# Expert part of a gated attention and mixture-of-experts kernel: eight row buffers, four bias buffers, transposes two tiles ahead

## The reference, cut to what matters

```
x = x + tanh(g_xattn) * gated_bidirectional_attention(layernorm(x), ctx)     # x: 8 x 512 x 512, float32
xt = layernorm(x).reshape(4096, 512)
probs = softmax(xt @ router_w + router_b)          # 8 experts
gate, idx = max(probs), argmax(probs)              # one expert for each token
y = gate * (xt @ expert_w[idx] + expert_b[idx])
out = x + tanh(g_ffn) * y
```

## Time and profile before

| | us |
|---|---|
| median of 3 runs | 1170.18 (1168.96 to 1170.37) |
| the profiled execution | 1162.84 |
| its span, first to last instruction | 1161.1 |
| PE busy | 1144.8 (99%) |
| DVE busy | 709.3 (61%) |
| ACT busy | 459.3 (40%) |
| POOL busy | 212.4 (18%) |

### The profile page before, as it was taken

The page is one execution under the profiler, slowest core; times in us unless marked ns, Lnnn a source line. Parts: engine busy times, 40 slices in busy tenths (PEclk is TensorE's granted clock), DMA queues, the critical chain, the costliest instruction groups (busy, mean ns, idle before and its releaser), DMA issues.

```text
span 1161.1 us, 18112 instructions
## 1 busy us (share of the span) xinstructions
PE 1144.8 (99%) x5933; PEld 942.6 (81%) x5933; DVE 709.3 (61%) x1494; ACT 459.3 (40%) x815; POOL 212.4 (18%) x339
## 2 busy tenths in 40 slices
PE   8999999999999999999999999999999999999988
PEld 6888888888888888888888888888888888877876
DVE  6666646564656555754576356546565658689655
ACT  5634413442344224432443134423342355554432
POOL 2400101020101100110011011101020101257754
PEclk9999999999999999999999999999999999999999
DMA  7141102010201020111101110103010312677783
GB/s 255 42 162 44 37 28 100 11 39 28 99 9 49 27 99 9 41 35 63 45 21 36 63 64 21 37 27 99 9 40 0 137 47 77 201 259 209 203 242 108
DMA packets 59444, 90.64 MB, mean 78 GB/s; under 512 B 20522, under 2 KB 21062, under 8 KB 59400
## 3 DMA queue, kind: packets, MB, share of 16 engines
q1 hardware_dynamic: 49232, 64.25, 18.2%
q0 software_dynamic: 7264, 19.20, 5.1%
q10 hardware_dynamic: 2904, 6.63, 1.6%
HBM read 62.77 MB, written 29.12 MB: 79 GB/s over the span
## 4 chain that ended last, share of the span: by engine, by line
PE 90%; issue 2%; SPq 2%; DMA 2%; DVE 2%; POOL 2%; ACT 1%; POOLq 0%; ACTq 0%; DVEq 0%
PE mm L160 59%; PE u L1049 15%; PE tr L1001 8%; PE u L160 5%; PE tr L160 1%; SPq L1579 1%; PE tr L1103 1%; DMA in_tile<-x_rows,u_row 1%; PE mm L1830 1%; SPq L1580 1%; POOL out L1659 1%; DMA probs<-in_L_ffn_expert_b 0%; DMA slot_as_f<-in_L_xattn_Wk_s 0%; DVE arena L1273 0%; DVE slot_as_f L1806 0%
## 5 line engine op out<-in xcount | busy, mean ns | idle before, releaser
L160 PE MATMUL mm<-arena 128*128 128x512 f32 x1536 | 374.1, 395 | 1.5 <-DVE arena L1273 1.4
L160 PEld LDWEIGHTS mm<-arena 128*128 128x128 f32 x1536 | 282.8, 188 | 58.5 <-DVE arena L1273 1.6
L1049 PE MATMUL u<-arena 128*128 128x512 f32 x768 | 189.8, 397 | 0.0
L160 PE MATMUL mm<-arena,q_pair 128*128 128x512 f32 x768 | 183.8, 394 | 0.0
L160 PEld LDWEIGHTS mm<-arena,q_pair 128*128 128x128 f32 x768 | 141.7, 188 | 28.7
L1049 PEld LDWEIGHTS u<-arena 128*128 128x128 f32 x768 | 140.0, 188 | 27.4
L1273 DVE TENSOR_TENSOR arena<-tr,arena 128x512 fp32r<-128x512 f32 x144 | 96.6, 685 | 36.9 <-ACT arena L1164 16.5
L1273 DVE TENSOR_TENSOR arena<-mm,arena 128x512 fp32r<-128x512 f32 x64 | 44.2, 691 | 91.4 <-ACT arena L1155 90.1
L1151 ACT ACTIVATE q_pair<-mm,c_col 128x512 fp32r<-128x512 f32 x64 | 44.1, 689 | 125.8 <-PE mm L160 122.6
L1274 DVE SCALAR_TENSOR_TENSOR q_pair<-mm,c_col,q_pair 128x512 fp32r<-128x512 f32 x64 | 48.1, 751 | 70.7 <-ACT q_pair L1151 69.0
L1155 ACT ACTIVATE arena<-mm 128x512 fp32r<-128x512 f32 x64 | 38.3, 599 | 128.8 <-PE mm L160 128.8
(11 more groups left out here) (220 smaller groups left out, 1555.8 us busy)
## 6 DMA issues: line engine op xcount, KB each, us to landing
in_tile<-in_ctx SPq DMA_DIRECT2D x31, 256.0 KB, 2.7
x_tile<-in_x SPq DMA_DIRECT2D x29, 256.0 KB, 2.6
x_rows<-x_tile SPq DMA_DIRECT2D x29, 256.0 KB, 2.1
in_tile<-in_x SPq DMA_DIRECT2D x28, 256.0 KB, 2.7
x_rows_early<-x_tile SPq DMA_DIRECT2D x28, 256.0 KB, 2.3
probs<-in_L_ffn_expert_b SPq DMA_DIRECT2D x21, 256.0 KB, 4.9
slot_as_f<-in_L_ffn_expert_w SPq DMA_DIRECT2D x4, 1024.0 KB, 5.5
slot_as_f<-in_L_ffn_expert_w ACTq DMA_DIRECT2D x3, 1024.0 KB, 7.5
```

Source lines behind the costliest of these rows:

```text
L160: last = pe.matmul(bank, lhsT(a, c), rhs(b, c), start=start and n == 0, stop=stop and n == C * len(PASSES) - 1)
L1049: last = pe.matmul(u_bank[m][:], v_pair[:, i % 2, a, tile(m)], pt_pair[:, i % 2, p], start=i == 0 and n == 0, stop=i == T - 1 and n == 2)
```

## The change

It does the following:

- Eight row buffers instead of six; the two new ones lie in `probs`, which the last batch frees with its M transposes. Four bias buffers instead of seven.
- PE transposes two tiles ahead: T(i) is transposes of i+2, then product i. In T0, T18 and T19 the transposes stand behind the product. Tile 1 is transposed in TP, ahead of the last gate product. ACT does high(i+2) and normalise(i+3), DVE low(i+2), add_bias(i), finish(i).
- POOL's gathers get an order of their own (`gathers_in_turn`): gather 6 behind scatter 1; in T2 and T3 two gathers each, in front of the scatter; then gather(i+7) up to T12; none in T13 to T15; one each in T16 and T17 (tiles 20, 21), two each in T18 to T20 (22 to 27), then again gather(i+7).
- The four list scatters of the last batch are issued in one go in RK0 (before: one there, three in steps of their own behind T10, T11 and T12). TB3 stands before T10, TB4 and TB5 before T11, TB6 and LI0 before T12.
- The late indices: four tiles in LI0, and then two tiles a step from T13, behind the step's bias (before: four a step from T15, ahead of it).
- ACT's wait for the last gate product moves from normalise(2) to the head of T0, ahead of high(1).

```
-ROWS, NORMED, PAIR, BIAS, BANK, OUT = 6, 3, 3, 7, 4, 4
+ROWS, NORMED, PAIR, BIAS, BANK, OUT = 8, 3, 3, 4, 4, 4
...
-               T6 LG1 LR1 NT2 NM3 NR2 T7 LG2 LR2 NT3 NR3 T8 LG3 LR3 RT0 IW0 T9 RK0 T10 TB3 RS1
-               T11 TB4 RS2 T12 TB5 RS3 TB6 LI0"""
+               T6 LG1 LR1 NT2 NM3 NR2 T7 LG2 LR2 NT3 NR3 T8 LG3 LR3 RT0 IW0 T9 RK0 TB3 T10 TB4 TB5
+               T11 TB6 LI0 T12"""
...
-                    for t in range(1 if after else T):
+                    for t in range(T):
                         scatter_list(t)
-                elif kind == "RS":
-                    scatter_list(i)
...
                 if i == 1:
-                    for n in range(3, BIAS):
-                        load_bias(n)
-                if FIRST_LATE < i:
-                    load_late_idx(i - FIRST_LATE)
+                    load_bias(3)
                 if i + BIAS - 1 == EARLY:
                     sp.wait_ge(experts_ready, 2)
                 if 0 < i <= TILES - BIAS:
                     load_bias(i + BIAS - 1)
+                if i >= FIRST_LATE:
+                    for n in range(2):
+                        if EARLY + LOADS + 2 * (i - FIRST_LATE) + n < TILES:
+                            load_idx(EARLY + LOADS + 2 * (i - FIRST_LATE) + n)
...
+            elif n == 6:
+                pool.wait_ge(attention.m_tr, 4 * B)
...
+        def gathers_in_turn(i):
+            if i < 2:
+                return ()
+            if i < 4:
+                return (2 * i + 3, 2 * i + 4)
+            if i < EARLY - ROWS + 1:
+                return (i + ROWS - 1,)
+            if i < EARLY - 4:
+                return ()
+            if i < EARLY - 2:
+                return (i + 4,)
+            if i < EARLY + 1:
+                return (2 * i - 14, 2 * i - 13)
+            return (i + ROWS - 1,) if i + ROWS - 1 < TILES else ()
...
-                if ROWS <= i + ROWS - 1 < TILES and i > 0:
-                    gather(i + ROWS - 1)
+                for n in gathers_in_turn(i):
+                    gather(n)
                 scatter(i)
+                if i == 1:
+                    gather(6)
...
             elif kind == "T":
-                if i + 1 < TILES:
-                    high(i + 1)
+                if i == 0:
+                    act.wait_ge(attention.g_mm, 4 * B)
+                    high(1)
+                    normalise(2)
                 if i + 2 < TILES:
-                    normalise(i + 2)
+                    high(i + 2)
+                if i + 3 < TILES:
+                    normalise(i + 3)
...
+                behind = i == 0 or EARLY <= i + 2 < EARLY + 2
...
-                if i + 1 < TILES:
-                    transpose_rows(i + 1)
+                if not behind and i + 2 < TILES:
+                    transpose_rows(i + 2)
...
+                if behind:
+                    transpose_rows(i + 2)
```

More of the change, by code:

```diff
@@ L46 @@
 EARLY = 20
-ROWS, NORMED, PAIR, BIAS, BANK, OUT = 6, 3, 3, 7, 4, 4
+ROWS, NORMED, PAIR, BIAS, BANK, OUT = 8, 3, 3, 4, 4, 4
 LOADS = 4
 SP_LOADS = 4
-FIRST_LATE = 14
+FIRST_LATE = 13
 FILLS = 5
@@ L1464, in scatter_list, with run @@
                 in_=token_ids[:, t:t + LINE], in_offset=None).then_inc(listed, 16)
-        def run(b, steps, after=False):
+        def run(b, steps):
             for kind, rel, d, i in steps:
@@ L1507, in gpsimd @@
             else:
-                run(B - 1, [step], after=True)
+                run(B - 1, [step])
     part = Part(sync, scalar, vector, gpsimd, tensor)
@@ L1555, in experts_part @@
     q, c2s, slot = k.pairs_as_f32[:, 0], k.pairs_as_f32[:, 1], attention.slot_of_gs
+    mix = attention.probs[:].rearrange("p t l -> p (t l)")
     def pair_in(whole, n):
@@ L1562, in experts_part @@
     row = [k.in_tile[:, 0], k.in_tile[:, 1], k.in_tile[:, 2], c2s[:, 4 * H:4 * H + ROWX],
-           c2s[:, 4 * H + ROWX:4 * H + 2 * ROWX], q[:, 5 * H:5 * H + ROWX]]
+           c2s[:, 4 * H + ROWX:4 * H + 2 * ROWX], q[:, 5 * H:5 * H + ROWX], mix[:, 0:ROWX], mix[:, ROWX:2 * ROWX]]
     y = [slot[:, n * H:(n + 1) * H] for n in range(OUT)]
-    bias = [c2s[:, 7 * H:8 * H], q[:, 7 * H:8 * H], slot[:, 7 * H:8 * H]] + [attention.probs[:, t] for t in range(T)]
+    bias = [c2s[:, 7 * H:8 * H], q[:, 7 * H:8 * H], slot[:, 7 * H:8 * H], mix[:, 2 * ROWX:2 * ROWX + H]]
     tr_bank, y_bank = attention.mm_bank, attention.u_bank
@@ L1581, in load_idx @@
                          ).then_inc(idx_loaded[n // LOADS], 16)
[L1583 to L1586, removed]
         def load_bias(n):
@@ L1628, in run @@
                 sp.wait_ge(attention.listed, 16 * T * B)
-                load_late_idx(0)
+                for n in range(EARLY, EARLY + LOADS):
+                    load_idx(n)
         return run
@@ L1683, in normalise @@
                 act.wait_ge(attention.gc_mm, 1)
-            elif n == 2:
-                act.wait_ge(attention.g_mm, 4 * B)
             elif n >= NORMED:
@@ L1700, in run @@
                 normalise(0)
+                normalise(1)
             elif kind == "TP":
                 high(0)
-                normalise(1)
             elif kind == "T":
-                if i + 1 < TILES:
-                    high(i + 1)
+                if i == 0:
+                    act.wait_ge(attention.g_mm, 4 * B)
+                    high(1)
+                    normalise(2)
                 if i + 2 < TILES:
-                    normalise(i + 2)
+                    high(i + 2)
+                if i + 3 < TILES:
+                    normalise(i + 3)
         return run
@@ L1814, in run @@
             elif kind == "T":
-                if i + 1 < TILES:
-                    low(i + 1)
+                if i == 0:
+                    low(1)
+                elif i + 2 < TILES:
+                    low(i + 2)
                 add_bias(i)
                 finish(i)
+                if i == 0:
+                    low(2)
         return run
@@ L1836, in run @@
                 transpose_rows(0)
+                transpose_rows(1)
             elif kind == "T":
+                behind = i == 0 or EARLY <= i + 2 < EARLY + 2
                 if i == 0:
```

## The result

The change makes the kernel slower. Beside each other on one chip, before took 1170.37 us (median of 5 runs, 1168.96 to 1171.34) and after 1175.77 us (5 runs, 1173.96 to 1178.26): a ratio of 1.0054, 95% interval 1.0039 to 1.0069. I had forecast 1169.0 us with a range of 1164.5 to 1172.6. The profiled execution of after took 1173.96 us, with a span of 1172.2.

What follows compares the result with a forecast made beforehand. PE was taken to bound the kernel, so only its gaps could be won. The terms -0.4 + 2.65 - 1.7 + 2.8 - 6.1 + 1.6 = -1.15 took 1170.18 to 1169.0 us, range 1164.5 to 1172.6.

Steps and rivals of the forecast that it cites:

- second half: From product 21 on: gathers asked for eight tiles ahead and evenly spaced biases remove the 6.1 us lost there, -6.1.
- T20: Ahead of tile 22's transposes: row 22 lands at 1093.05, PE waits 2.8 us, +2.8; row 20 comes just in time.
- Start and T1 to T5: Tile 1 transposed earlier, -0.4; early gathers on POOL delay BS1, NM1 and T5's transposes, +2.65.
- Table stretch: Low part made a tile earlier on DVE, so PE's 0.3 and 1.15 us gaps go: -1.7.
- Clock: Two new PE gaps over 2 us, near 1036 to 1039 and at 1091; one drop of the granted clock taken, +1.6.
- Rival 4: At T20 gathers 22 and 23 land late, PE waits 6.2 us, both new gaps lower the clock: 1174.0, chance 0.15.
- I take the difference over unchanged: The runs' median lies 7.3 us above the profiled execution; this was assumed the same after: 1170.18 - 1.15 = 1169.0.

Runs made afterwards that it cites:

- b_again: The kernel before, unchanged, run and profiled again: 1159.95 us, 0.9995 of before, span 1158.4.
- a_again: The kernel after, unchanged, run again beside the kernel before: 1.0036 of before, span 1163.3.
- b_third: The kernel before, unchanged, profiled a third time, in a session where it runs near 1170 us: 1.0005 of before, span 1168.5.
- a_fourth: The kernel after, unchanged, a fourth time, in a session with before near 1170 us: 1.0065 of before, span 1173.3.
- a_one_ahead: The kernel after with transposes, high and low parts one tile in advance as before, all the rest of the change kept: 1.0006 of before.
- a_back_to_one: The kernel after, but nothing transposed at T16 and one tile in advance again from T17 on: 1.0071 of before.
- b_lists_once: The kernel before with late indices two a step behind the bias, list scatters in one go and the table's parts one step earlier: 0.9983 of before.

## Why the prediction was wrong

When PE starts the transposes ahead of a product, in two pairs of profiles (b_again and a_again are from two sessions with before near 1160, b_third and a_fourth from one near 1170):

```
ahead of product       3       5      12      13      17      22      36     span
b_again            1029.9  1037.3  1063.9  1067.1  1081.4  1097.4  1144.9  1158.4
a_again            1030.4  1041.8  1067.8  1071.0  1083.8  1105.4  1150.3  1163.3
after - before        0.5     4.5     3.9     3.9     2.4     8.0     5.4     4.9
b_third            1031.0  1038.4  1067.2  1072.6  1089.2  1106.3  1155.0  1168.5
a_fourth           1031.4  1043.2  1071.2  1079.7  1094.4  1115.3  1160.3  1173.3
after - before        0.4     4.8     4.0     7.1     5.2     9.0     5.3     4.8
```

From product 3 on, after has one more tile's transposes behind it than before; the differences hold some 0.5 us for that, which the last column gives back. The difference of the spans is the same in both, 4.8 to 4.9. Two steps of the prediction failed: the size of the second half (-6.1, read from one execution), and T20, where row 20 was said to be just in time and the transposes behind the product were taken as free. Term by term, with the first pair and clock drops (1.6 each) taken out:

- **Start and T1 to T5**: forecast -0.4 + 2.65 = +2.25, measured 4.5 - 1.6 = +2.9. BS1's end was right to 0.1 us, and a_one_ahead shows that chain alone holding PE for 2.23 us. But in after it is not what PE waited for. Row 6 took 6.7 us (6.6 in a_again), above the 6 up to which I had said it hides; PE stood for it, and product 4 then covered NM1's delay. That the wait for row 6 came out as long as the one forecast for tile 7 is luck. The 0.52 us ahead of tile 3 were not in the sum.
- **Table stretch**: forecast -1.7, measured 2.4 - 4.5 = -2.1. Right in these sessions. In the pair of 1170 it was +0.4, eaten by the late answer behind the four list scatters.
- **T20**: forecast +2.8, measured 8.0 - 2.4 - 1.6 = +4.0. The step that failed here is "row 20 comes at 1086 to 1087.5 and just in time". The starts were written at 1072.8 instead of 1070.0, SP's first late index left at 1073.8 instead of 1070.7, bias 15 stood behind four of them and held DVE 2.48 us, so scatter 15 went at 1084.8 and gather 20 behind it at 1086.1 instead of 1082.65. Its row came at 1090.8. That is a chain that I had written down, with each link some 3 us too early. Of the +4.0, 1.8 are the wait for row 20 and 1.4 the change of order ahead of tile 22, which the sum had at nothing; the 2.8 forecast for row 22's landing did not come, the row was in time.
- **Clock**: one drop forecast, two here (three in the first profile): +1.6 more.
- **Second half**: forecast -6.1, measured 4.9 - 8.0 = -3.1, of which 0.5 are the transposes done in advance. This is the largest miss. The mechanism is right: from tile 23 on after has no gap in a_again. But there was no 6.1 to be won: from product 20 to the end b_again loses 2.7 us. I had sized the term from one execution, which had 2.25 and a clock drop at tile 30, where b_again has 0.90, b_third 1.31, and neither a drop.

The sum of the differences is 0.65 - 0.4 + 1.2 + 1.6 + 3.0 = 6.05, which takes -1.15 to +4.9.

Rival 4 came nearest (1174.0): slower, at T20, with the clock. Its mechanism, late double gathers, is not what the runs show. Row 20, which PE waits for in a_again, is gathered by itself, and the first row of a double gather, row 22, is in time. a_one_ahead has the same gathers and no gap at either place, because two tiles of lookahead want each row 3.2 us sooner and because it has no change of order. I priced the lookahead as cover for DVE (-1.7) and never as a demand on rows, but for tile 22. No run goes two tiles in advance with the change of order taken out, so what each of the two costs in time is read from gaps, not measured. Where it was taken back (a_one_ahead against a_again, each against before) the difference is 1.0036 to 1.0006, some 3.5 us; where it was added alone, +5.7.

The step "I take the difference over unchanged" between profile and median also deserved doubt. The profile of before lay 7.3 us under its median, that of after 1.8: the first had no late answers and the runs, by b_third, usually do. It happens that this cancels in the difference of typical executions (4.8 and 4.9), but comparing the two first profiles, 11.1 us apart, would have doubled the effect.

What stays open: what holds the answers in some sessions. Shown is that they come only there (in seven of the eight profiles with before near 1170, the first one of before being the exception, and in none of the twelve others), that the one behind the list scatters is 6.3 to 6.7 us in all four profiles with the lists in one go and no pause, and that it was 2.1 us in the one profile with a pause of POOL. That POOL's descriptors are what the signals wait behind is an inference. The Trainium skill, "Perfetto Trace Analysis", section "Tensor Engine Instruction (MATMUL, LD_WEIGHTS)", says that a matmul's end in a profile is an estimate and that its semaphore update leaves only when the write to PSUM is acknowledged; a late signal would so be invisible on PE's own rows, as here. No run shows whether it is the signal or its delivery that is late.

## What to carry to other kernels

Lookahead on an engine is bought from whoever feeds it: before adding a stage in advance, move every input's due time forward by one step and see which is then late, above all the one at the end of the longest chain. Where a step moves its share from ahead of another to behind it and back, write out the order on the neighbouring engine at the step of the return: here it held PE for 1.39 us with every input in time. A gain read from one gap in one execution should be checked against a second profile and against the distance between that profile and the median; here the gap with the clock drop behind it was the part that did not come again. When a change has several parts and one queue's order is among them, try that alone first: two late indices a step behind the bias gave 0.9982 alone, where all the parts together made the kernel slower.

## Not expected of the hardware

In sessions where the kernel before runs near 1170 us, ACT and DVE start up to 8.3 us after the PE work that they wait for, in both kernels. In after, a_fourth and a_back_to_one the late answer behind the list scatters ended 1.3 to 1.4 us after POOL had issued the last of an unbroken row of indirect DMAs (1074.96 and 1076.26, 1076.92 and 1078.31, 1075.08 and 1076.51), but in b_lists_once 0.2 us after (1073.40 and 1073.57), so the distance is no rule; in a_again POOL's row was as unbroken from 1063.2 to 1077.4, and ACT answered within 0.04 us:

```profile
1068.62 0.96 POOL L1462 DMA_INDIRECT token_lists<-token_ids,slot_i  x1 [0.30 <-issue]
1069.89 0.98 POOL L1650 DMA_INDIRECT in_tile<-x_rows_early,u_row  x1 [0.30 <-issue]
```

```profile
1071.61 0.60 ACT L1709 ACTIVATE c2s_pair<-mm 128x512 fp32r<-128x512 f32 x1 [1.89 <-PE mm L1852]
```

Whether the clock falls behind a gap is not settled by the gap's length alone: in a_again it fell behind 2.73 and 1.78 us (the next products took 4.58 and 4.61), in a_one_ahead it held behind 2.23 (mean granted clock 1.000).
